# Four gather buffers and fewer TensorE signals in the message passes of a two-part graph network

## The reference

```
m      = relu(x[src] + ea) + 1e-7
logits = m * t
mx     = segment_max(logits, dst);  e = exp(logits - mx[dst])
agg    = segment_sum(m * e / segment_sum(e, dst)[dst], dst)
x      = x + mlp(agg + x)          # per node: matmul, layernorm, relu, matmul
```

## Time and profile before

| | |
|---|---|
| median of 3 runs | 11325.51 us (11321.66 to 11331.46) |
| the profiled execution | 11249.37 us |
| its span | 11247.6 us |
| granted TensorE clock, mean over the span | 0.682 |
| busy share of the span | POOL 61%, DVE 53%, PE 46%, ACT 27% |

### The profile page before, as it was taken

One profiled execution on the slowest core, in us unless ns is written; L12 is line 12 of the kernel. 1 busy time (PEld: TensorE's weight loads), 2 busy tenths in 40 slices (PEclk: granted clock), 3 DMA queues, 4 the chain that ended last, 5 costly groups with the idle time before them and its releaser, 6 DMA issues. The chain is left out here.

```text
span 11247.6 us, 87085 instructions
## 1 busy us (share of the span) xinstructions
PE 5127.0 (46%) x22750; PEld 3577.1 (32%) x22750; DVE 5980.2 (53%) x8070; ACT 3007.5 (27%) x4424; POOL 6815.3 (61%) x6468
## 2 busy tenths in 40 slices
PE   2444444443333332433333334333333358888887
PEld 2333323332222222322222223222222245555554
DVE  4443434443445444535444444444454458888887
ACT  1323223233233232323232323233332331111110
POOL 5554555545656666456666564656566538888887
PEclk8666566666666666666666666665666669999998
DMA  5332333332333333323333332233333335555554
GB/s 137 108 101 97 110 99 99 110 117 57 100 94 104 95 102 87 103 69 104 95 102 97 94 105 76 85 96 103 94 104 95 99 89 97 96 92 97 96 94 83
DMA packets 780499, 1091.38 MB, mean 97 GB/s; under 512 B 501054, under 2 KB 543664, under 8 KB 778660
## 3 DMA queue, kind: packets, MB, share of 16 engines
q1 hardware_dynamic: 453902, 862.82, 22.4%
q0 software_dynamic: 322624, 224.55, 14.1%
q10 hardware_dynamic: 3916, 3.40, 0.1%
HBM read 610.39 MB, written 479.85 MB: 97 GB/s over the span
## 5 line engine op out<-in xcount | busy, mean ns | idle before, releaser
L730 POOL DMA_INDIRECT xg<-h_tab,idx x4968 | 4765.1, 959 | 3546.9 <-DVE idx L988 1870.3
L988 DVE COPY idx<-idx_full 128x24 int32 x208 | 37.6, 181 | 4040.2 <-ACT zl L895 4022.3
L800 PE MATMUL turn<-ident,den 128*128 128x128 f32 x2592 | 492.2, 334 | 3307.1 <-ACT st_all L903 3170.1
L1293 POOL DMA_INDIRECT acc<-vm,tgt x1026 | 1597.6, 1557 | 374.1 <-issue 299.6
L891 ACT ACTIVATE u<-zl,attrB 128x512 f32<-128x512 f32 (+1 forms) x672 | 746.5, 1122 | 3347.6 <-remote 2720.9
L800 PEld LDWEIGHTS turn<-ident,den 128*128 128x128 f32 x2592 | 393.0, 221 | 3357.2 <-ACT st_all L903 3214.9
L785 PEld LDWEIGHTS zl<-ident,xg 128*128 128x128 f32 x5184 | 971.7, 254 | 1122.5 <-issue 993.5
L785 PE MATMUL zl<-ident,xg 128*128 128x128 f32 x5184 | 980.8, 336 | 609.7 <-issue 506.0
L781 PE MATMUL zl<-ea,attrW 128*128 128x512 f32 (+1 forms) x1008 | 752.6, 840 | 793.9 <-DVE rx L1001 751.2
L903 ACT ACTIVATE st_all<-turn 128x512 f32<-128x512 f32 (+1 forms) x1344 | 746.8, 577 | 494.7 <-PE turn L800 324.6
L1542 DVE TENSOR_TENSOR spreadz<-turn,hi_hot 128x2560 f32<-128x2560 f32 x270 | 762.7, 2825 | 65.0 <-ACT gh L1427 26.0
(11 more groups left out here) (259 smaller groups left out, 7340.9 us busy)
## 6 DMA issues: line engine op xcount, KB each, us to landing
sums<-st_all SPq DMA_DIRECT2D x208, 1536.0 KB
ea<-feat SPq DMA_DIRECT2D x158, 768.0 KB
srcB<-src_flat SPq DMA_DIRECT2D x108, 768.0 KB
rp<-run_pen SPq DMA_DIRECT2D x210, 384.2 KB
xg<-h_tab,idx POOLq DMA_INDIRECT x4968
run_head<-zeros SPq DMA_DIRECT2D x216, 192.0 KB
hd<-run_head SPq DMA_DIRECT2D x108, 384.0 KB
ea<-in_edge_attr_dram SPq DMA_DIRECT2D x104, 384.0 KB
```

The costliest lines, as they stand in the source:

```text
L730: g_.indirect_dma_start(xg[b][:, k, h, :], None, h_tab[:, :], bass.IndirectOffsetOnAxis(ap=idx[b][:, h, k:k + 1] if small is None else idx ...
L800: ins = pe.transpose(ps[6 + (b + r) % 2][:, j * P:(j + 1) * P], sum_v[:, gr * gt + j, :], ident[:, :])
L1293: g_.indirect_dma_start(acc[i][:, :], bass.IndirectOffsetOnAxis(ap=tgt[b][:, t_:t_ + 1], axis=0), vm[b][:, t_, :], None, compute_op=ALU.ad ...
```

## The change

The gathered rows and their indices get DEPTH = 4 buffers in place of 2; `idx_full` is longer by two windows, the indices copied by VectorE are those of window g+4, and GpSimd's wait for a free buffer is for `z_ps` of window g-4, once a window and no longer ahead of each group. The parity `b` of all else stays. To find the room, five temporary lists of the start share memory with `segmax`, `den` and `num`, and VectorE waits ahead of each `den` scan for the stores of these lists (five stores in all, made once, at the start). The semaphores of the node gathers are those of the row gathers.

TensorE now increments `z_ps` once a window (after the third group), `at_ps` twice (after groups 1 and 2; group 0 has none), `back_ps` three times (after every second group). ScalarE waits for these: it copies turned features as two groups in one instruction and then the third, starts all three `u` after the one `z_ps`, and copies the turned sums in pairs, with one `back_sb` for a pair. `back` waits for a pair of banks and no longer for a single one.

```diff
-        xg_in = [[sem(f"xg_in{i}_{gr}") for gr in range(NG)] for i in range(2)]
+        xg_in = [[sem(f"xg_in{i}_{gr}") for gr in range(NG)] for i in range(DEPTH)]
...
-            idx = [sb(f"idx{i}", [P, 2, K], I32, c) for i in range(2)]
+            idx = [sb(f"idx{i}", [P, 2, K], I32, c) for i in range(DEPTH)]
...
-            BU = 2 * NG
+            BU, AU = NG, 2
...
                         for k in range(NG * gt):
-                            if k % gt == 0:
-                                g_.wait_ge(z_ps, NG * g + k // gt + 1 - NG * 2 + Z0)
+                            if k == 0:
+                                g_.wait_ge(z_ps, g + 1 - DEPTH + Z0)
                                 g_.sem_inc(gather_go, 1)
...
                         for gr in range(NG if first else 0):
-                            pe.wait_ge(at_sb, NG * g + gr + 1 - 2 + A0)
                             if gr == 0:
+                                pe.wait_ge(at_sb, AU * g + A0)
                                 pe.wait_ge(back_sb, BU * (g - 1) + BS0)
+                            if gr == NG - 1:
+                                pe.wait_ge(at_sb, AU * g + 1 + A0)
...
-                            ins.then_inc(at_ps, 1)
+                            if gr:
+                                ins.then_inc(at_ps, 1)
...
-                            ins.then_inc(z_ps, 1)
+                        ins.then_inc(z_ps, 1)

                     def back(g, b, gt=GT):
-                        for r in range(BU):
+                        for r in range(2 * BU):
...
-                            pe.wait_ge(back_sb, BU * g + max(r - 1, 0) + BS0)
+                            if r % 2 == 0:
+                                pe.wait_ge(back_sb, BU * g + r // 2 + BS0)
...
-                            ins.then_inc(back_ps, 1)
+                            if r % 2:
+                                ins.then_inc(back_ps, 1)
...
-                        for gr in range(NG if isinstance(l, int) else 0):
-                            a.wait_ge(z_ps, NG * (g - 1) + gr + 1 + Z0)
-                            a.wait_ge(at_ps, NG * g + gr + 1)
+                        banks = turn.rearrange("p (g c) -> p g c", g=2)
+                        for n, (gr, count) in enumerate(((0, 2), (2, 1)) if isinstance(l, int) else ()):
+                            a.wait_ge(z_ps, g + Z0)
+                            a.wait_ge(at_ps, AU * g + n + 1)
...
+                        a.wait_ge(z_ps, g + 1 + Z0)
                         for gr in range(NG):
-                            a.wait_ge(z_ps, NG * g + gr + 1 + Z0)
...
-                        for r in range(BU):
+                        for r in range(2 * BU):
                             gr, s_ = r % NG, r // NG
-                            a.wait_ge(back_ps, BU * g + r + 1 + BP0)
+                            if r % 2 == 0:
+                                a.wait_ge(back_ps, BU * g + r // 2 + 1 + BP0)
...
+                            if r % 2:
+                                ins.then_inc(back_sb, 1)
...
                         if width == W:
-                            next_lists(w + 2, b)
+                            next_lists(w + DEPTH, place)
...
                         v.wait_ge(back_ps, BU * (g - 1) + BP0)
+                        v.wait_ge(out_lists, 16 * 5)
```

More of the change, by code:

```diff
@@ L474, in gnn @@
         with ExitStack() as c:
-            xg.append(sb("xg1", [P, K, 2, D], F32, c))
+            xg += [sb(f"xg{i}", [P, K, 2, D], F32, c) for i in range(1, DEPTH)]
             ea = [sb(f"ea{i}", [P, 2, K, D], F32, c) for i in range(2)]
@@ L592, in load @@
                     def load(g, w, b, first):
-                        sp.wait_ge(z_ps, NG * g + NG - NG * 2 + Z0)
+                        sp.wait_ge(z_ps, g + 1 - 2 + Z0)
                         if first:
@@ L734, in layer @@
                     def layer(l):
-                        if isinstance(l, int):
-                            window(1, 1, l, 1)
-                        else:
+                        if not isinstance(l, int):
                             g_.wait_ge(tab_out, 16 * MC * l + 16)
                             g_.sem_inc(gather_go, 1)
[L740 to L744, removed]
+                        for b in range(1 if isinstance(l, int) else 0, DEPTH):
+                            window(l * LW + b, b, l, b)
+                        with g_.Fori(1, FULLW // DEPTH) as i:
+                            for b in range(DEPTH):
+                                window(l * LW + DEPTH * i + b, DEPTH * i + b, l, b)
                         g_.wait_ge(idx_last_in, 16 * LAST_LISTS)
                         for s in range(LAST):
-                            window(l * LW + FULLW + s, None, l, s % 2, GT // 2, s)
+                            window(l * LW + FULLW + s, None, l, s, GT // 2, s)
                         for b in range(2):
@@ L978, in _ @@
                     v.wait_ge(idx_full_in, 32)
-                    for b in range(2):
+                    for b in range(DEPTH):
                         v.tensor_copy(idx[b].rearrange("p h k -> p (h k)"), lists[:, b * 2 * K:(b + 1) * 2 * K]).then_inc(idx_ok, 1)
@@ L988, in next_lists, with window @@
                         v.tensor_copy(idx[b].rearrange("p h k -> p (h k)"), lists[:, bass.ds(w * 2 * K, 2 * K)]).then_inc(idx_ok, 1)
-                    def window(g, w, i, l, b, width=W):
+                    def window(g, w, i, l, b, place, width=W):
                         link = Chain(v, dve_step, g * STEPS)
@@ L1083, in _ @@
                         v.tensor_scalar(tcur[:, 1:2], tcur[:, 0:1], EPS, None, ALU.mult).then_inc(tcur_ok, 1)
-                        with v.Fori(0, FULL_PAIRS) as i:
-                            for b in range(2):
-                                window(l * LW + 2 * i + b, 2 * i + b, i, l, b)
+                        with v.Fori(0, FULLW // DEPTH) as i:
+                            for n in range(DEPTH):
+                                window(l * LW + DEPTH * i + n, DEPTH * i + n, DEPTH // 2 * i + n // 2, l, n % 2, n)
                         for s in range(LAST):
-                            window(l * LW + FULLW + s, FULLW + s, FULL_PAIRS + s // 2, l, s % 2, W // 2)
+                            window(l * LW + FULLW + s, FULLW + s, FULL_PAIRS + s // 2, l, s % 2, None, W // 2)
                         v.wait_ge(dve_step, (l + 1) * LW * STEPS)
```

81 lines of the change are left out of this document (41 added, 40 removed).

## The result

| | before | after |
|---|---|---|
| median of 4 runs each, one chip | 11328.49 us | 11945.74 us (11942.85 to 11946.45) |
| ratio, 95% interval | | 1.0542 [1.0528, 1.0555] |
| span of the profiled execution | 11247.6 us | 11944.2 us |

What follows compares the result with a forecast made beforehand. Bound: POOL's 30.1 us of gathers plus its wait behind TensorE's held logits signal. Steady windows -547, heads +40, layer 0 nothing: -507 us, 10,742 profiled, 10,818 as median; own range 10,350 to 11,230, 8 in 10 10,150 to 11,600.

Steps and rivals of the forecast that it cites:

- The bound: Steady layer 1: 38.1 us a window, 30.1 of gathers, the rest a chain behind TensorE's held logits signal.
- One signal for the logits: Layers 1 to 3: late `u` cost 2.3 us, but the signal at 15.7 passes at once, logits at 20.8.
- third rival: The one logits signal waits for POOL's pause: 40.6 us a window, +510 us, 11,835; chance 0.20.
- 10.1 us a signal: Price of each TensorE signal during POOL's 60.2 us run, taken from releases in a two-window run of the earlier trace.
- 34.3 us a window: Steady windows of layers 1 to 3, against 38.1 before: 144 windows, -547 us (ends -979 and +58).
- Layer 0: Windows of 44.2 us: no change, from -6 to +2.3 us a window, -290 to +110 in all.
- Heads of layers: Start of layers 1 to 3: third window's logits some 13 us later, +40 us (-75 to +165).
- Four buffers: Gather buffers: nothing off POOL's 30.1 us, no change of rhythm alone; they let POOL's pause go.
- The lists' stores: VectorE's added wait ahead of `den`: nothing; at most one window, 44 us, once.
- POOL's floor: Fewer signals are not held, so POOL's 30.1 us is the window: -1248 us, 10,080; chance 0.12.
- 26 ns a signal: Skill's rule on semaphore increments by matmuls: dropped signals worth some 0.15 us a window, 30 us in all.

Runs made afterwards that it cites:

- Point 3: GpSimd stops ahead of its 13th gather until the logits signal of the window three before: changed kernel, 10902.98 us; four buffers with nine signals, 10856.60 us.
- point 6: Changed kernel plus 1024-column memsets behind every second gather in layers 1 to 3 and two GpSimd stops in layer 0: 11541.01 us, ratio 1.0245.
- Point 2: Changed kernel with SyncE's transfers after the logits signal, ratio 1.0500; with GpSimd's group waits restored, 1.0566; with seven added signals nobody waits for, 1.0554.
- point 1: Changed kernel with GpSimd held to two windows ahead, 11990.22 us; four buffers with the nine and twelve signals of before, 11338.45 us.

## Why the prediction was wrong

- **The bound** was read rightly: the late signal of the logits, on a chain through `u`, the index copy and GpSimd's run. Point 3 breaks that chain by one wait and is 3.7% faster than before; point 6 shows the hold and its absence in one trace.
- **The step that failed**: "*One signal for the logits.* ... The gain is that the one signal falls at 15.7, with none just ahead of it ... and so I take it as passing at once". The kernel after ends the logits at the same distance from the run's start (16.0 us in the window shown), and the signal waits for the pause, in window after window, 34.1 us after the start of the run. I had laid the delay to other signals ahead of it. The kernel after faults that by itself: nothing stands just ahead of this signal. Point 2 adds that seven signals behind it change nothing. The earlier trace rows had it in one line: the signal of 15.7 arrived with the pause, and the one before it passed on its own. By these rows what counted was how long GpSimd had been issuing when the signal was made, which the prediction wrote down as its third rival and gave 0.20. It is not a fixed limit: in the run of before that starts at 4516.27 a signal made after 15.5 us was taken up after 16.7.
- **What followed from it**: GpSimd's run never became 60 us, so the 10.1 us a signal of the earlier trace rows were never used (they also hold the round of copy and turn already, which the sum adds once more). 34.3 us a window was forecast, 40.0 came.
- ***Layer 0***, which the forecast put at no change, is the second term that failed: +266.4 us, 5.1 a window. ScalarE waits for the turned features as long as before, but from their release to GpSimd's next gather it is 11.1 us before (1024.11 to 1035.21) and 16.1 after (1228.74 to 1244.80). The merged turned features lose the early group 0 of the earlier trace rows and start their copy, 1.02 us long, only after the pause; the next turn, copy and logits are all behind it.
- **Rival 3's own sum** was near in total and wrong in its parts. Layers 1 to 3: 156 x 2.5 = 390 against 277 measured. Layer 0: +2.3 a window, the late `u` alone, against 5.1.
- ***Heads of layers***, +40 forecast: no such cost shows. The first 12 windows of a layer, from first gather to first gather, take 447.1 us before and 450.1 to 451.7 after, 3 to 5 more, where steady windows at 40.1 in place of 37.9 would give 27 more; GpSimd now gathers five windows in one run there. What the sum had nothing for are +110 between the layers and +43 behind the last gather; the four buffers alone give 97 and 44 (point 1). That GpSimd's greater lead only moves time there out of the layers is likely and was not tested.
- ***Four buffers*** "take nothing off" and "alone ... change no rhythm": right, 37.8 us a window with nine signals. ***The lists' stores*** at nothing: no window of the trace shows the wait, and no run tested it alone.
- **POOL's floor**, 0.12, is what the chip shows in other sessions (30.2 us a window), but there for the kernel before as well, within 0.03%.
- The 26 ns a signal that the prediction cites from the Trainium skill (page "TensorE: Matmul & The Clock Gate", section "The cost: per-tile semaphore tail") can't be told from nothing here: in point 2, 7 x 26 ns x 208 windows would be 38 us, 0.0033 of the ratio, if all of it were on the path; the ratios with and without the seven, 1.0554 and 1.0542, have intervals that overlap. The delay of 18.2 us is another thing than this price.

## What to carry to other kernels

While GpSimd issues indirect DMAs back to back, a signal of TensorE may be held until it pauses or slows, however few signals there are: ask how long the series is when the signal is made, and what stands behind the last signal, before you merge early signals into it. Break such a series with a real pause; a wait that is always met makes none (point 2), while a stop that waits for the very signal that is held gained 4%, and stops of this kind lost nothing where nothing was held. And measure in more than one session before a mechanism of the chip is called the kernel's bound: here one kernel had two times 19% apart.

## What was not expected of the hardware

- The kernel before takes 11,275 to 11,328 us in four sessions and 9,127 to 9,137 in three; one chip gave both. In the second kind no signal was late in the traces read.
- Where signals are held, they land about 4 us after 24 gathers in a row (4.0 to 4.3 in the kernel after, mostly 3.7 to 4.2 before), be it at a window's end or in its middle, and 6.0 us after the series between two layers; the signals in the first 12 us of a run pass at once. In layer 1 before, the second group, ended 13 to 15 us into the run, was taken up anywhere from 16.7 to 29.9 us in the 45 windows of the earlier trace rows. I have no mechanism for this. A simple queue that drains in order would not hold an early signal to the end of the run, and what differs between two sessions was not found (the mean granted clock of the kernel before is 0.67 to 0.68 in the one kind and 0.70 to 0.73 in the other, which may as well follow from the hold).
- How small a gap or how slow a pace suffices is open: the 0.30 us between gathers doesn't, 1 us more after every second one does. So is whether layer 0's stops alone help where signals are held; both would bear on the best kernel. The best that was run there is four buffers with nine signals and the stop, 10856.60 us.
